# An attention layer over an adjacency matrix: own scales for parts of ks_t and x, scores begun on 1024 rows, bounds of x taken during the fill, adj loaded one group at a time

## The reference

```python
scores = jnp.einsum('nd,md->nm', qs, ks)          # qs is x
scores = jax.nn.leaky_relu(scores, negative_slope=0.2)
scores = jnp.where(adj > 0, scores, NEG_BIG)
attn = jax.nn.softmax(scores, axis=1)
x = _layernorm(x + jnp.einsum('nm,md->nd', attn, ks), axis=-1)
```

## Time and profile before

| | us |
|---|---|
| median of the 3 timed runs | 1582.51 |
| the profiled execution, its own time | 1580.71 |
| its span, first to last instruction | 1578.5 |
| first `score` matmul | 29.5 |
| first mask (group 0) | 34.48 |
| first `weigh` matmul | 88.48 |

### The profile page before, as it was taken

One profiled execution on the slowest core, in us unless ns is written; L12 is line 12 of the kernel. 1 busy time (PEld: TensorE's weight loads), 2 busy tenths in 40 slices (PEclk: granted clock), 3 DMA queues, 4 the chain that ended last, 5 costly groups with the idle time before them and its releaser, 6 DMA issues.

```text
span 1578.5 us, 42464 instructions
## 1 busy us (share of the span) xinstructions
PE 1516.8 (96%) x16576; PEld 1429.4 (91%) x16576; DVE 1494.1 (95%) x1788; ACT 1441.6 (91%) x1810; POOL 1440.3 (91%) x1237
## 2 busy tenths in 40 slices
PE   1699999999999999999999999999999999999997
PEld 1489999999999999999999999999999999999997
DVE  6999999999999999999999999999999999999993
ACT  4599999999999999999999999999999999999997
POOL 1699999999999999999999999999999999999997
PEclk9999999999999999999999999999999999999999
DMA  9754555555555555555545555545555545555520
GB/s 357 271 214 173 191 191 190 186 188 191 179 196 196 179 182 198 179 190 198 187 171 198 192 180 196 197 167 194 196 181 188 198 175 191 191 193 178 193 88 8
DMA packets 67799, 296.33 MB, mean 188 GB/s; under 512 B 6160, under 2 KB 32784, under 8 KB 34832
## 3 DMA queue, kind: packets, MB, share of 16 engines
q1 hardware_dynamic: 67600, 293.63, 53.0%
HBM read 289.41 MB, written 4.19 MB: 186 GB/s over the span
## 4 chain that ended last, share of the span: by engine, by line
PE 91%; issue 2%; POOL 2%; DMA 1%; DVE 1%; SPq 1%; ACT 0%; ACTq 0%; DVEq 0%; POOLq 0%
PE weighted L644 28%; PE scores L610 13%; PE scores L611 13%; PE scores L612 13%; PE weighted L660 7%; PE weighted L656 7%; PE weighted L658 7%; DMA ring<-in_x_t 1%; DVE running L532 1%; PE floors L629 1%; POOL pt_lo L316 1%; POOL ring L312 1%; DMA adj_sb<-in_adj 1%; SPq L235 0%; PE running L619 0%
## 5 line engine op out<-in xcount | busy, mean ns | idle before, releaser
L312 POOL TENSOR_TENSOR ring<-ring,floor 128x768 f32<-128x768 f32 (+2 forms) x512 | 780.5, 1525 | 65.4 <-ACT floor L413 65.4
L517 DVE SCALAR_TENSOR_TENSOR ring<-adj_sb,scores 128x1024 f32<-128x1024 int32 x512 | 622.8, 1217 | 30.4 <-ACT scores L390 27.5
L390 ACT ACTIVATE scores<-scores,shrink 128x1024 f32<-128x1024 f32 x512 | 554.5, 1083 | 106.1 <-PE scores L612 101.8
L316 POOL TENSOR_TENSOR pt_lo<-ring,pt_hi 128x512 f16<-128x512 f32 x512 | 596.5, 1165 | 17.3 <-ACT pt_hi L402 14.1
L610 PE MATMUL scores<-xt_hi,kt_hi 128*128 128x256 f16 x2048 | 559.0, 273 | 48.2 <-DVE xt_lo L482 29.5
L396 ACT ACTIVATE ring<-ring,lift 128x1024 f32<-128x1024 f32 x512 | 583.3, 1139 | 1.4 <-POOL ring L312 0.9
L612 PE MATMUL scores<-xt_hi,kt_lo 128*128 128x256 f16 x2048 | 559.7, 273 | 0.0
L611 PE MATMUL scores<-xt_lo,kt_hi 128*128 128x256 f16 x2048 | 559.5, 273 | 0.0
L532 DVE TENSOR_TENSOR running<-ring,running 128x1024 f32<-128x1024 f32 x448 | 547.8, 1223 | 0.1
L644 PE MATMUL weighted<-k_rows,ring 128*128 128x129 f32 x4096 | 544.8, 276 | 2.2 <-DVE y L569 1.3
L644 PEld LDWEIGHTS weighted<-k_rows,ring 128*128 128x128 f32 x4096 | 497.6, 191 | 14.4 <-ACT ring L396 9.9
(11 more groups left out here) (54 smaller groups left out, 439.8 us busy)
## 6 DMA issues: line engine op xcount, KB each, us to landing
adj_sb<-in_adj SPq DMA_DIRECT2D x256, 1024.0 KB, 4.8
ring<-in_ks_t SPq DMA_DIRECT2D x8, 512.0 KB, 6.6
ring<-in_x_t SPq DMA_DIRECT2D x8, 512.0 KB, 12.9
xt_raw<-in_x_t SPq DMA_DIRECT2D x32, 128.0 KB, 4.9
x_row<-in_x SPq DMA_DIRECT2D x32, 128.0 KB, 4.8
out<-normed SPq DMA_DIRECT2D x32, 128.0 KB, 5.1
k_rows<-in_ks SPq DMA_DIRECT2D x16, 128.0 KB, 3.2
ring<-in_ks SPq DMA_DIRECT2D x1, 2048.0 KB, 9.3
```

Of the source, the lines that this page charges most:

```text
L312: nc.gpsimd.tensor_tensor(here, here, below, ALU.subtract).then_inc(gap_ready, 1)
L316: nc.gpsimd.tensor_tensor(pt_lo[:, g % PARTS, :, :], ring[:, g % RING, WHOLE:, :], pt_hi[:, g % PARTS, :, :], ALU.subtract).then_inc(part_ ...
L517: nc.vector.scalar_tensor_tensor(ring[:, g % RING, :, :], adj_sb[:, n % ADJS, half * QUAD:(half + 1) * QUAD, :], 0.0, scores[:, g % 2, :, ...
```

## The change

- **Scales.** Six scales instead of two. Three sets of ks_t (columns 0 to 1023, 1024 to 4095, the rest), one for the ks rows (`K_ALL`), one for the first three blocks of x (`X_FIRST`), one for the other blocks (`X_ALL`). `bend` undoes the product of the two scales that apply (`shrink` has a column for each set). The reduction over partitions moves from POOL to PE and DVE: `magnitudes` multiplies the column, broadcast, with the identity, and `most` takes the maximum along the row and makes scales. It is done in four stages: before slot 0, around slot 0, in slots 4 to 6, and in slots 32 to 34.
- **Start.** Scores begin once three blocks of x and the first 1024 columns of ks_t are there. Splits of ks_t are now 16 units of 512 columns. Units 0 to 2 have their low half on DVE, the others on POOL, and ACT's high halves stand in slots 0 to 12, three slots ahead of use. ACT bounds six of the eight ks_t loads, three of them in slots 1 to 3.
- **x.** The 4 MB of `x_t` are bounded later, in 16 parts of 512 columns (256 KB), all on ACT (`bound_x`), in slots 11 to 20. There are two buffers, lent by `normed` and `x_row`. SP issues a part when the part two before it is bounded, in the slot in which that one is bounded. The x rows themselves are loaded in slot 22.
- **adj.** Loads of one group (0.5 MB) in six buffers instead of two groups (1 MB) in three; the host lays adj out to match.
- **SP.** `ks_raw` and then `k_rows` are issued ahead of slot 0, right behind six adj loads. `high_rows` is cut into quarters in slots 7 to 10.

```diff
-    LOAD = 2
-    ADJS = 3
+    ADJS = 6
     WHOLE = 2
     PARTED = QUAD - WHOLE
     PARTS = 3
     STEP = 1024
     STEPS = M // STEP
-    EARLY = 4
+    PART_X = 2 * BLOCK
+    STEPS_X = N // PART_X
+    X_FIRST, K_SETS, K_ALL, X_ALL, SCALES = 0, (1, 2, 3), 4, 5, 6
+    FIRST_BLOCKS = 3
+    CUTS = (0, 1, 4, STEPS)
+    STAGES = ((0, 2), (2, 3), (3, 5), (5, 6))
+    MAGNITUDES = (4, 6, 8, 9)
+    SCALE_STEPS = 5
+    DVE_UNITS = 3
...
+        x_parts = [normed.rearrange("p a j d -> p (a j d)"), x_row.rearrange("p a j d -> p (a j d)")]
...
+        def unit(u):
+            return slice(u * QUAD * P, (u + 1) * QUAD * P)
...
+        def k_set(u):
+            return sum(u * QUAD * P >= c * STEP for c in CUTS[1:])
+        def x_set(b):
+            return int(b >= FIRST_BLOCKS)
...
+        def bound_slot(c):
+            return c + 11 if c < 2 else 12 + c // 2 if c < 14 else c + 5
...
+                wait(sp, masked_ready, n - ADJS + 1)
+                b, j = divmod(n, GROUPS)
+                sp.dma_start(adj_sb[:, n % ADJS, :, :], adj[b, j, :, :, :]).then_inc(adj_loaded[n % ADJS], 16)
+            def load_x_part(c):
+                if c == 1:
+                    sp.wait_ge(mag_step, 2)
+                wait(sp, mag_x_ready, c - 1)
+                sp.dma_start(x_parts[c % 2], x_t[:, c * PART_X:(c + 1) * PART_X]).then_inc(x_part_loaded[c % 2], 16)
...
             load_xt(0)
-            for n in range(ADJS):
+            load_xt(1)
+            sp.dma_start(x_parts[1][:, 0:BLOCK], x_t_v[2, :, :]).then_inc(x_third_loaded, 16)
+            for c in range(4):
+                load_ks_t(c)
+            for n in range(3):
                 load_adj(n)
-            load_xt(1)
-            sp.wait_ge(scale_step, SCALE_STEPS)
+                load_ks_t(n + 4)
+            load_ks_t(STEPS - 1)
+            for n in range(3, ADJS):
+                load_adj(n)
+            sp.dma_start(ks_raw.rearrange("p (j t) d -> p j t d", t=PARTED), ks_v[:, :, WHOLE:QUAD, :])\
+                .then_inc(ks_raw_loaded, 16)
             for j in range(GROUPS):
                 sp.dma_start(k_rows[:, j, :, 0:D], ks_v[:, j, 0:WHOLE, :]).then_inc(k_rows_loaded, 16)
-            sp.dma_start(ks_raw.rearrange("p (j t) d -> p j t d", t=PARTED), ks_v[:, :, WHOLE:QUAD, :])\
-                .then_inc(ks_raw_loaded, 16)
-            load_x(0)
-            load_x(1)
             for s in SLOTS:
                 b = whole(s, AT_STORE)
                 if b is not None:
                     store(b)
-                if s % LOAD == 1 and s // LOAD + ADJS < ALL // LOAD:
-                    load_adj(s // LOAD + ADJS)
+                if s + ADJS < ALL:
+                    load_adj(s + ADJS)
+                for c in range(STEPS_X):
+                    if s == (bound_slot(c - 2) if c > 1 else 8):
+                        load_x_part(c)
...
-            for column, count in ((1, STEPS + 1), (0, MAG_STEPS)):
-                pool.wait_ge(mag_step, count)
-                nc.gpsimd.partition_all_reduce(mag_all[:, column:column + 1], mag[:, column:column + 1], P,
-                                               bass.bass_isa.ReduceOp.max).then_inc(mag_all_ready, 1)
...
+            for u in range(DVE_UNITS, GROUPS):
+                low_ks_t(u)
+                if u == 9:
+                    split_x(1)
...
+            def bound_ks_t(c, n):
+                act.wait_ge(ks_t_loaded[c], 16)
+                wait(act, mag_k_bounded, n)
+                nc.scalar.activation(junk, ks_t_raw[:, c * STEP:(c + 1) * STEP], ACT.Abs,
+                                     accum_out=mag_k[:, c:c + 1]).then_inc(mag_k_bounded, 1)
             def bound_x(c):
-                cols = slice(c * STEP, (c + 1) * STEP)
-                act.wait_ge(x_t_loaded[c], 16)
-                nc.scalar.activation(x_t_raw[:, cols], x_t_raw[:, cols], ACT.Abs, accum_out=mag_x[:, c:c + 1])\
+                act.wait_ge(x_part_loaded[c % 2], 16 * (c // 2 + 1))
+                nc.scalar.activation(x_parts[c % 2], x_parts[c % 2], ACT.Abs, accum_out=mag_x[:, c:c + 1])\
                     .then_inc(mag_x_ready, 1)
...
+            bound_ks_t(1, 0)
             split_x(0)
-            for c in range(EARLY, STEPS):
-                split_ks_t(c)
-            split_x(1)
-            act.wait_ge(scale_step, SCALE_STEPS)
+            split_ks_t(0)
+            split_ks_t(1)
+            bound_ks_t(2, 1)
+            bound_ks_t(4, 2)
...
+                if b == 0:
+                    act.wait_ge(scale_step, SCALE_STEPS * (k + 1))
+                elif b == FIRST_BLOCKS and u == 0:
+                    act.wait_ge(scale_step, SCALE_STEPS * len(STAGES))
+                nc.scalar.activation(here, here, ACT.Prelu, scale=shrink[:, x, k:k + 1], alpha=SLOPE)\
...
+                if s == 0:
+                    split_ks_t(2)
+                if s < 5:
+                    split_ks_t(s + 3)
+                if 1 <= s < 4:
+                    bound_ks_t(s + 4, s + 2)
+                if 5 <= s < 13:
+                    split_ks_t(s + 3)
                 if s == 6:
-                    high_rows()
+                    split_x(1)
+                if 7 <= s < 11:
+                    high_rows(s - 7)
+                for c in range(STEPS_X):
+                    if s == bound_slot(c):
+                        bound_x(c)
...
+            def most(stage):
+                at = slice(*STAGES[stage])
+                many = at.stop - at.start
+                start = SCALE_STEPS * stage
+                if stage < 3:
+                    spread_out = floors.rearrange("p a n -> p (a n)")[:, 0:many * P]
+                else:
+                    spread_out = running[:, 2, 0:many * P]
+                dve.wait_ge(mag_spread_ready, stage + 1)
+                nc.vector.tensor_reduce(mag_all[:, at], spread_out.rearrange("p (c m) -> p c m", c=many), AX.X, ALU.max)\
+                    .then_inc(mag_all_ready, 1)
+                dve.wait_ge(mag_all_ready, stage + 1)
...
+                if s == 0:
+                    split_ks_t(2)
+                if s == 4:
+                    dve.wait_ge(mag_k_bounded, 6)
+                    magnitude(mag[:, K_SETS[2]:K_SETS[2] + 1], mag_k[:, CUTS[2]:CUTS[3]])
+                    magnitude(mag[:, K_ALL:K_ALL + 1], mag_k[:, :])
+                if s == 5:
+                    most(2)
+                if s == 32:
+                    dve.wait_ge(mag_x_ready, STEPS_X)
+                    magnitude(mag[:, X_ALL:X_ALL + 1], mag_x[:, :])
                 b = whole(s, AT_LOWEST)
                 if b is not None:
                     lowest(b)
...
+                    if b == 1:
+                        most(3)
...
+            def magnitudes(stage, to):
+                pe.wait_ge(mag_step, MAGNITUDES[stage])
+                wait(pe, mag_all_ready, stage)
+                first, end = STAGES[stage]
+                for i, column in enumerate(range(first, end)):
+                    mine = mag_k[:, 0:1] if column == K_SETS[0] else mag[:, column:column + 1]
+                    last = nc.tensor.matmul(to[:, i * P:(i + 1) * P], mine.to_broadcast([P, P]), eye[:, :],
+                                            start=True, stop=True)
+                last.then_inc(mag_spread_ready, 1)
...
-        "in_adj": np.ascontiguousarray(adj.reshape(n // 256, 256, m // 1024, 8, 128).transpose(0, 2, 4, 3, 1)),
+        "in_adj": np.ascontiguousarray(adj.reshape(n // 256, 256, m // 512, 4, 128).transpose(0, 2, 4, 3, 1)),
```

More of the change, by code:

```diff
@@ L126, in adj_attention_layernorm @@
         ks_t_loaded = [sem(f"ks_t_loaded{c}") for c in range(STEPS)]
-        x_t_loaded = [sem(f"x_t_loaded{c}") for c in range(STEPS)]
+        x_part_loaded = [sem(f"x_part_loaded{j}") for j in range(2)]
+        x_third_loaded = sem("x_third_loaded")
         k_rows_loaded = sem("k_rows_loaded")
@@ L204, in _, with load_ks_t @@
         def _(sp):
-            for c in range(STEPS):
+            def load_ks_t(c):
                 cols = slice(c * STEP, (c + 1) * STEP)
                 sp.dma_start(ks_t_raw[:, cols], ks_t[:, cols]).then_inc(ks_t_loaded[c], 16)
-            for c in range(STEPS):
-                cols = slice(c * STEP, (c + 1) * STEP)
-                sp.dma_start(x_t_raw[:, cols], x_t[:, cols]).then_inc(x_t_loaded[c], 16)
             def load_adj(n):
-                wait(sp, masked_ready, LOAD * (n - ADJS + 1))
-                b, h = divmod(n, GROUPS // LOAD)
-                sp.dma_start(adj_sb[:, n % ADJS, :, :], adj[b, h, :, :, :]).then_inc(adj_loaded[n % ADJS], 16)
+                wait(sp, masked_ready, n - ADJS + 1)
[6 more added lines that the diff above has]
+                sp.dma_start(x_parts[c % 2], x_t[:, c * PART_X:(c + 1) * PART_X]).then_inc(x_part_loaded[c % 2], 16)
             def load_xt(b):
@@ L284, in split_x @@
                 here = xt_raw[:, b % 2, :]
-                nc.gpsimd.tensor_scalar(here, here, scale_x, 1.0, ALU.mult, ALU.mult).then_inc(xt_scaled_ready, 1)
```

(35 more changed lines are left out.)

176 lines of the change are left out of this document (91 added, 85 removed).

## The result

The changed kernel takes 1587.35 us (median of 10 runs, 1585.66 to 1589.04), the kernel before 1582.29 us on the same chip (10 runs, 1580.48 to 1583.13). The ratio is 1.0034, its 95% interval 1.0024 to 1.0044: slower by 0.34%, more than can be taken for noise. I had forecast 1582.2 us and no difference. The profiled executions took 1587.38 us (span 1585.6) and 1580.71 us; that pair lies 6.7 us apart against 5.06 of the medians, since the profiled one of before lies 1.6 us under its median. I account for the 7.1 us between the two spans.

What follows compares the result with a forecast made beforehand. PE bounds the kernel (512 slots at 2.89 us), so only the first `weigh` counts. Start -1.6, clock 1.3, rest 0 give -0.3 us on the profiled 1580.71; with the median 1.80 above that execution, 1582.2 us, range 1576.5 to 1588.0.

Steps and rivals of the forecast that it cites:

- mask 6: Fill: it waits for its adj load, queued behind ks_raw and k_rows, and starts at about 36.4 us.
- masks 6 to 13: Fill after the adj stall: DVE sets the pace, seven slots of 2.26 us, 15.8 us in all.
- mask 13 to 14: First wait for the parts of x: part 3 is issued behind adj 18, so about 5.0 us.
- masks 14 to 19: Fill slots paced by loads of x's parts through two buffers: 3.9 us each, 19.5 us.
- mask 19 to 20: End of the fill: bound of part 14, copy of `floor`, bend, DVE's gaps and minimum, 5.0 us.
- clock, to the second `weigh`: PE's clock, low after waits, delays slots 8 to 10 and the first `weigh`: 0 to 3 us, taken as 1.3.
- last scale: Slots 32 to 34: three more DVE steps, about 1.1 us, and one matmul; cost 0, at most 1.1 us.
- a slot [...] I take 3.9: Late fill: bound, issue and landing of x's parts make a slot 3.9 us, within 3.3 and 4.3.
- the second loop: Late fill: a loop over two slots with the adj load ahead of the parts, 7.7 us, 3.85 each.
- rival D: Late fill: transfers land 0.4 us later, slots of 4.3, clock 1.7 us more: 1586.3 us; chance 0.20.
- DVE paces again: seven slots of 2.26: Fill behind the adj stall: DVE alone sets the pace and brings mask 13 to 52.2 us.
- SP issues the 16 `k_rows` loads in 8.06 us [...] and has the time: Start: SP's issuing of these loads does not delay adj 6; the transfers ahead of it do, 7.3 us for `k_rows`.

Runs made afterwards that it cites:

- e6: Changed kernel without its last scale; x blocks from the fourth on use the scale of the first three: 1586.57 us, ratio 1.0031 to the kernel before.
- e8: Changed kernel with one buffer instead of two for the parts of x: 1609.52 us, ratio 1.0173 to the kernel before.
- e1: Changed kernel without the loads of x's parts 2 to 15; ACT bounds the first two again and again: 1574.41 us, ratio 0.9947 to the kernel before.
- e3: Changed kernel with eight buffers instead of two for x's parts, loads issued up to six parts earlier: 1574.14 us, ratio 0.9946 to the kernel before.
- e11: Changed kernel with ACT's four conversions of ks_raw in slots 12 to 15 instead of 7 to 10: 1586.80 us, ratio 1.0025 to the kernel before.

## Why the prediction was wrong

Where the time is (traces, against my steps):

| step | forecast | measured | error |
|---|---|---|---|
| mask 6 | 36.4 | 38.24 | +1.8 |
| masks 6 to 13 | 15.8 | 17.66 | +1.9 |
| mask 13 to 14 | 5.0 | 4.84 | -0.2 |
| masks 14 to 19 | 19.5 | 21.71 | +2.2 |
| mask 19 to 20 | 5.0 | 5.49 | +0.5 |
| clock, to the second `weigh` | 1.3 | 1.5 | +0.2 |
| last scale | 0 | 0.8 | +0.8 |

The sum of errors is 7.2 us. With the -0.3 us forecast it makes 6.9, and the spans differ by 7.1. The measured column is one execution. In e6, with the same fill, mask 6 is at 38.98, mask 13 to 14 takes 6.65 us and mask 20 is at 90.05, so single rows may be off by a microsecond or two, and that the row of mask 13 to 14 fits is partly luck.

Right: the bound (PE's slot, still 2.89 us from the second `weigh` on), so that only the first `weigh` counts; both places where the fill waits and what releases it (a DMA of adj at mask 6; ACT idle 12.4 us before L413, against some 11); that the parts of x eat a lead of 17 to 19 us (I left 1.6 of it, and in fact mask 20 came 4.65 us later than before); the price of the clock.

Wrong, first and largest: "a slot [...] I take 3.9". This is the term that was mis-sized: the load of a part took 3.8 us in the median, where I took 2.85, and a slot 4.34, which at mask 19 is 2.2 us. A part does take 2.65 us when alone (part 5, issued at 59.76), but an adj load of 0.5 MB is ahead of it in most turns, and I had put that only into the second loop. In the chain above, a part issued 0.4 us behind an adj load took 4.93 us, those issued 1.2 to 1.3 behind one 3.8 and 4.0, and those 1.6 and 2.7 behind one 3.3 and 3.4. e8 shows the short value at its place: 2.6 to 3.2. The slot was 4.34, above the 4.3 from which rival D, at 1586.3 us, was to decide. I gave it 0.20. Its first half, transfers that land later, happened; its second, 1.7 us more for the clock, did not (0.2), and the terms below stood in its place, so that its time is near the measured one is partly luck. e1 and e3 show what the turn costs in all: without it 13 us are gone.

Second: "DVE paces again: seven slots of 2.26". In slots 7 to 10 ACT paced at 2.65. The three durations were at hand; I added ACT's work only for slots 13 to 18. e11 confirms the mechanism, though little of it arrives.

Third: mask 6. ks_raw landed at 28.69 where my sum gives 27.7, and the 16 k_rows loads took 8.2 us instead of 7.3. Within the 3 us that I allowed, but in the same direction as the rest. And "SP issues the 16 `k_rows` loads in 8.06 us [...] and has the time" did not hold. SP's timeline has them last 23.11 us, and adj 6 is issued only behind them. The chain goes through these issues and not through the transfer ahead:

```profile
10.32 23.11 SPq L286 DMA_DIRECT2D k_rows<-in_ks  x16
```
```profile
32.96 0.47 SPq L286
33.43 0.04 issue
33.48 4.67 DMA adj_sb<-in_adj
```

The DMA engines are full beside it (share 1.21 from 28 to 33.5 us), so whether the issues or the transfers set the 8.2 us stays open; no run separates them.

Fourth: "The last scale [...]: 0, at most 1.1". It cost 0.8 (e6). I argued that DVE catches up; but the wait is passed on at once, since PE turns the floors in the same slot. And DVE's part was 2.1 us rather than 1.1, of which 1 us is the product that ends with POOL's instruction (seen in the trace, tested by no run).

None of these alone turns the sign beyond 0.2%; four small errors on the same side did. What the first, the second and the last have in common: I took the durations of single steps, left out what else stood in the same slot or queue, and let the fill follow the faster of two paces.

Between the 7.1 us of the spans and the 5.06 of the medians lie 1.6 us, by which the profiled execution of before is under its median, and 0.4, since the changed kernel has 1.8 us outside its span and the one before 2.2. What stays open: which rows of the table carry these 2 us, and whether the 1.1 us by which e11 is nearer to the kernel before than the change is (3.9 us slower against 5.1) are real.

## What to carry to other kernels

A lead won at the start is worth only what the narrowest place behind it lets through: add up each engine's work and each buffer's turn (use, semaphore, issue, landing) in every slot of the fill, before summing the gain. The length of a small load counts with what stands ahead of it in the queue, and more buffers hid it here at no cost in bytes (e3). When a wait for a DMA shows, look at the GB/s beside it: at 224 more buffers helped; at 382, near the 411 that the start of before reached, fewer bytes are left to try, which no run here does.
